# Row sums of the attention weights from two matmuls in place of three, in a two-layer cross-attention kernel

## What is computed

```python
# layer 0
scores = einsum('bqh,bkh->bqk', Q, K) * scale
x = query + einsum('bqh,hd->bqd', softmax(scores, -1) @ V, Wo) + bo
# layer 1: softmax over the QUERY axis (axis=1), so the rows of w do not sum to one
w = softmax(einsum('bte,bme->btm', q, k) * scale, axis=1)
pred = einsum('btm,bme->bte', w, v)          # v = latent @ Wv + bv
x = pred + emb
out = (x - mu) * rsqrt(var + EPS) * gamma + beta
```

## Time and profile before

| | |
|---|---|
| median of 3 runs | 1209.86 us (1209.61 to 1211.09) |
| the profiled execution's own time | 1209.69 us |
| its span, first to last instruction | 1207.9 us |
| mean granted TensorE clock | 0.982 |
| PE busy | 1159.0 us, 96% of the span |
| DVE busy | 883.6 us, 73% |
| ACT busy | 858.5 us, 71% |
| POOL busy | 968.5 us, 80% |

### The profile page before, as it was taken

One profiled execution on the slowest core, in us unless ns is written; L12 is line 12 of the kernel. 1 busy time (PEld: TensorE's weight loads), 2 busy tenths in 40 slices (PEclk: granted clock), 3 DMA queues, 4 the chain that ended last, 5 costly groups with the idle time before them and its releaser, 6 DMA issues.

```text
span 1207.9 us, 25274 instructions
## 1 busy us (share of the span) xinstructions
PE 1159.0 (96%) x7985; PEld 1078.0 (89%) x7985; DVE 883.6 (73%) x2061; ACT 858.5 (71%) x1736; POOL 968.5 (80%) x772
## 2 busy tenths in 40 slices
PE   6969999999999999999999999999999999999983
PEld 5659999999999999999999999999999999999873
DVE  0346787778777777777787778777877787777763
ACT  1436777777777777777777777777777777777752
POOL 1335888898889888988898889888888988898764
PEclk8989999999999999999999999999999999999997
DMA  8235666676667666766666666666666666676431
GB/s 347 68 117 187 227 212 219 216 238 204 223 210 238 201 224 216 231 203 226 218 224 206 228 221 220 212 226 226 212 218 215 237 207 223 209 243 201 155 123 53
DMA packets 131839, 250.09 MB, mean 207 GB/s; under 512 B 15712, under 2 KB 89440, under 8 KB 123232
## 3 DMA queue, kind: packets, MB, share of 16 engines
q1 hardware_dynamic: 130800, 248.64, 61.6%
q10 hardware_dynamic: 1008, 1.06, 0.2%
HBM read 165.68 MB, written 83.95 MB: 207 GB/s over the span
## 4 chain that ended last, share of the span: by engine, by line
PE 93%; DMA 2%; DVE 1%; ACT 1%; POOL 1%; issue 1%; ACTq 0%; POOLq 0%; DVEq 0%
PE bank L314 90%; PE bank L392 2%; DMA beta_b<-in_beta 1%; PE bank L429 1%; PE bank L423 1%; ACT bank L502 0%; DVE scol L826 0%; DVE stats L847 0%; PE bank L442 0%; DMA gT<-g_dram 0%; POOL PT_lo L954 0%; POOL Y L1010 0%; POOL yT_lo L954 0%; DVE R L839 0%; ACTq L507 0%
## 5 line engine op out<-in xcount | busy, mean ns | idle before, releaser
L954 POOL TENSOR_TENSOR xT_lo<-IN,xT_hi 128x1024 fp32r<-128x1024 f32 x64 | 154.3, 2411 | 27.9 <-ACT xT_hi L502 27.9
L954 POOL TENSOR_TENSOR yT_lo<-yT_raw,yT_hi 128x1024 fp32r<-128x1024 f32 x64 | 152.4, 2381 | 28.0 <-ACT yT_hi L502 26.6
L1010 POOL TENSOR_TENSOR Y<-Y,gamma_b 128x512 f32<-128x512 f32 x128 | 162.9, 1295 | 0.9 <-ACT Y L636 0.9
L1013 POOL TENSOR_TENSOR Y<-Y,beta_b 128x512 f32<-128x512 f32 x128 | 163.1, 1298 | 0.0
L636 ACT ACTIVATE Y<-R,nmr,rstd 128x512 f32<-128x512 f32 x128 | 97.5, 809 | 80.8 <-POOL nmr L1002 80.8
L1000 POOL TENSOR_TENSOR rstd<-ve,half 128x2 f32<-128x2 f32 x64 | 44.8, 700 | 133.1 <-DVE nmu L862 133.1
L314 PE MATMUL bank<-yT_hi,A_hi 128*128 128x256 f32 x512 | 145.5, 284 | 5.3 <-POOL yT_lo L954 5.3
L314 PE MATMUL bank<-xT_hi,A_hi 128*128 128x256 f32 x512 | 145.5, 284 | 0.0
L314 PE MATMUL bank<-xT_hi,A_lo 128*128 128x256 f32 x512 | 145.3, 284 | 0.0
L314 PE MATMUL bank<-yT_lo,A_hi 128*128 128x256 f32 x512 | 145.2, 284 | 0.0
L314 PE MATMUL bank<-xT_lo,A_hi 128*128 128x256 f32 x512 | 145.0, 283 | 0.0
(11 more groups left out here) (108 smaller groups left out, 4252.1 us busy)
## 6 DMA issues: line engine op xcount, KB each, us to landing
IN<-in_packed SPq DMA_DIRECT2D x64, 1024.0 KB, 4.9
R<-in_x SPq DMA_DIRECT2D x64, 512.0 KB, 4.4
y_dram<-y_blk SPq DMA_DIRECT2D x256, 128.0 KB, 2.6
yT_raw<-y_dram SPq DMA_DIRECT2D x64, 512.0 KB, 3.7
out<-Y SPq DMA_DIRECT2D x64, 512.0 KB, 2.6
E_dram<-E_blk SPq DMA_DIRECT2D x256, 64.0 KB, 1.8
PT_raw<-E_dram SPq DMA_DIRECT2D x64, 256.0 KB, 2.8
gT<-g_dram SPq DMA_DIRECT2D x64, 128.0 KB, 3.7
```

The lines of the kernel that those rows point to most:

```text
L954: return nc.gpsimd.tensor_tensor(dst, src, fp(hi), ALU.subtract)
L1010: nc.gpsimd.tensor_tensor(y[:, q, :], y[:, q, :], gamma_b[:, :], ALU.mult).then_inc(Y_mul, 1)
L1013: last = nc.gpsimd.tensor_tensor(y[:, q, :], y[:, q, :], beta_b[:, :], ALU.add)
```

## The change

The row sum over keys is `w_hi[0] + w_lo[0] + w_hi[1] + w_lo[1]`. The changed kernel adds the full weights of the two key tiles first and splits this sum once. ACT writes `w_1` (the weights of tile 1, not rounded); DVE computes `w_sum` = tile 0 times its reciprocal + `w_1`; ACT rounds `w_sum` to `w_sums_hi`; POOL subtracts to give `w_sums_lo`; PE's `s_` multiplies ones by these two. POOL's `w_low_sum` is gone. Besides, steps change places: `C_h` goes ahead of `wc_h` on ACT; on DVE `x2(r-1, 0)` goes ahead of `g_blocks`, `stats_ready` ahead of `rz1_`, and `x1(r+2, 1)` ahead of `w_l`; on POOL `cT_l` goes ahead of `scales`.

```diff
@@ PE @@
                 first(pe, s_set, n.count(back=1))
-                pe.wait_ge(w_los_set, n.count())
-                for t, part in enumerate((w[0][:, 0, :], w[0][:, 1, :], w_los[:, :])):
-                    last = nc.tensor.matmul(s_bank[:, 0:S], ones[:, :], part, start=(t == 0), stop=(t == 2))
+                pe.wait_ge(w_sums_lo, n.count())
+                for t, part in enumerate(w_sums):
+                    last = nc.tensor.matmul(s_bank[:, 0:S], ones[:, :], part[:, :], start=(t == 0), stop=(t == 1))
                 last.then_inc(s_full, 1)
@@ ACT @@
+            def w_1_(n):
+                if not n.there():
+                    return
+                act.wait_ge(rz1_set, n.count())
+                first(act, w_sum_set, n.count(back=1))
+                copy(w_1[:, :], S1_bank[:, S:2 * S], scale=rz1[:, 1:2]).then_inc(w_1_set, 1)
+
+            def w_sums_h(n):
+                if not n.there():
+                    return
+                act.wait_ge(w_sum_set, n.count())
+                first(act, s_full, n.count(back=1))
+                copy(w_sums[0][:, :], w_sum[:, :]).then_inc(w_sums_hi, 1)
...
                 if prefix:
+                    C_h(r.plus(3))
                     wc_h(r.plus(-1))
                     pred_seed_(r.plus(-1))
                     PT_h(r.plus(2))
                     u_h(r.plus(3))
-                    C_h(r.plus(3))
                 xT_h(r.plus(4))
...
                 w_h(r)
+                w_1_(r)
                 cT_h(r.plus(4))
+                w_sums_h(r)
                 normalise(r.plus(-1))
@@ DVE @@
+            def w_sum_(n):
+                if not n.there():
+                    return
+                dve.wait_ge(w_1_set, n.count())
+                dve.wait_ge(w_hi, n.count())
+                first(dve, w_sums_lo, n.count(back=1))
+                nc.vector.scalar_tensor_tensor(w_sum[:, :], S1_bank[:, 0:S], rz1[:, 0:1], w_1[:, :], ALU.mult, ALU.add
+                                               ).then_inc(w_sum_set, 1)
...
+                x2(r.plus(-1), 0)
                 g_blocks(r.plus(1))
-                x2(r.plus(-1), 0)
...
+                stats_ready(r.plus(-1))
                 rz1_(r)
-                stats_ready(r.plus(-1))
                 E0_blocks(r.plus(3))
                 variances(r.plus(-1))
                 x1(r.plus(2), 0)
+                w_sum_(r)
+                x1(r.plus(2), 1)
                 w_l(r)
-                x1(r.plus(2), 1)
@@ POOL @@
-            def w_low_sum(n):
-                if not n.there():
-                    return
-                pool.wait_ge(w_lo, n.count())
-                first(pool, s_full, n.count(back=1))
-                nc.gpsimd.tensor_tensor(w_los[:, :], fp(w[1][:, 0, :]), fp(w[1][:, 1, :]), ALU.add
-                                        ).then_inc(w_los_set, 1)
+            def w_sums_l(n):
+                if not n.there():
+                    return
+                pool.wait_ge(w_sums_hi, n.count())
+                minus(w_sums[1][:, :], w_sum[:, :], w_sums[0][:, :]).then_inc(w_sums_lo, 1)
...
+                cT_l(r.plus(4))
                 scales(r.plus(-1))
-                cT_l(r.plus(4))
-                w_low_sum(r)
+                w_sums_l(r)
```

More of the change, by code:

```diff
@@ L113, in build @@
         gT = sb("gT", [P, 1, S])
-        w_los = sb("w_los", [P, S], f32r)
+        w_1 = sb("w_1", [P, S])
+        w_sum = sb("w_sum", [P, S])
+        w_sums = split("w_sums", [P, S])
         scol = sb("scol", [P, ST, 32])
@@ L154, in build @@
         S1_seed, S1_full, nmax1_set, E1_set = sem("S1_seed"), sem("S1_full"), sem("nmax1_set"), sem("E1_set")
-        rz1_set, w_hi, w_lo, w_los_set = sem("rz1_set"), sem("w_hi"), sem("w_lo"), sem("w_los_set")
+        rz1_set, w_hi, w_lo = sem("rz1_set"), sem("w_hi"), sem("w_lo")
+        w_1_set, w_sum_set = sem("w_1_set"), sem("w_sum_set")
+        w_sums_hi, w_sums_lo = sem("w_sums_hi"), sem("w_sums_lo")
         s_full, s_set = sem("s_full"), sem("s_set")
```

## The result

The changed kernel takes 1230.39 us (median of 4 runs, 1228.81 to 1231.03), against 1209.92 for the kernel before (4 runs). The ratio is 1.016, with a 95% interval of 1.0145 to 1.0175: slower by 1.6%. The profiled execution took 1230.26 us, its span is 1228.5 us.

The account below looks back on a forecast made before the run. PE was taken as the bound, never waiting in mid-run, in 59 periods of 17.36 us. 1209.7 - 7.5 + 59 * 0.47 = 1229.9, +1 for the end: 1231 us, range 1210 to 1240.

Parts of the forecast that it names:

- The late seeds: Before `pred_`: scales 1.6 us late delay `vT`, `scol` and seeds; PE stalls 0.45 to 0.53 us a period, 0.47 taken.
- Waits that hang on one anchor do not add: Stalls before `wc_` and `pred_` both hang on `S0_`; the `w_lo` wait lies inside the 0.47 us.
- The late `w_lo`: Before `wc_`: `w_l` behind the second `x1` alone stalls PE 0.11 to 0.35 us a period, 0.26 taken, 0.20 possible.
- `PT_l` as a third chain: Before `Pc_`: later `Y` and `finish` delay `PT_l`; stall of 0.21 to 0.45 us, inside the seeds' stall.
- The price of the matmul: In `s_`: one of three matmuls goes in each of 64 sequences, 0.117 us each, saving 7.5 us.
- The number of periods and the end: 59 periods of 0.47 us stall each, and 1 us more in the last four sequences without a next sequence as cover.
- Only the matmul counts: Rival: the chain over `scales` has room, seeds arrive in time; 1202 us, stall below 0.12 us a period; chance 0.12.
- Only `w_l` stalls PE: Rival: POOL's order is harmless, PE waits before `wc_` only, 0.20 to 0.26 us a period; 1215 to 1219 us; chance 0.12.
- the fourth rival: Stalls of 0.1 to 0.17 us a period nearly cancel the gain; 1207.4 to 1212.3 us; chance 0.06.
- The clock: Rival: PE's pauses lower its clock, 2 us of each period at 1.2 GHz; about 1290 us; chance 0.02.

Follow-up runs that it names:

- 1: The changed kernel with POOL running `scales` ahead of `cT_l` again: 1221.25 us, ratio 1.0088.
- 8: The kernel before with `cT_l` ahead of `scales` on POOL and the added copy `w_1` on ACT, its result unused: 1232.33 us, ratio 1.0183.
- 9: The changed kernel with the copy `w_1` on ACT made twice, the first into an unread buffer: 1253.6 us, ratio 1.0359.
- 4: The changed kernel with `C_h` put back behind `u_h` on ACT: 1230.58 us, ratio 1.0165.
- 2: The changed kernel with `w_l` ahead of the second `x1` on DVE, behind `w_sum_`: 1231.65 us, ratio 1.0166.
- 3: The changed kernel with `scales` first on POOL and `w_l` ahead of the second `x1` on DVE: 1205.74 us, ratio 0.996.
- 11: The changed kernel with every step in the order of the kernel before, `w_l` directly behind `w_sum_`: 1205.87 us, ratio 0.9962.
- 6: The kernel before with `w_l` behind the second `x1` on DVE: 1214.28 us, ratio 1.0024.
- 5: The kernel before with `cT_l` ahead of `scales` on POOL: 1214.19 us, ratio 1.0025.
- 7: The kernel before with `cT_l` ahead of `scales` on POOL and `w_l` behind the second `x1` on DVE: 1213.44 us, ratio 1.0022.

## Why the prediction was right

**The forecast.** 1231 us was said, 1230.39 measured; slower by 1.7% was said, 1.6% measured. The period was to be 17.24 + 0.47 = 17.71 us; it is 17.69. The mechanism holds; that the total is as close as 0.6 us is luck in part (see the sizes below).

**The late seeds.** Right in every link. With the shift of 8.26 us, predicted and measured starts: `cT_hi` 603.04 and 603.04, `cT_lo` 603.76 and 603.77, `rstd` 605.02 and 605.03, `vT_hi` 607.44 to 607.52 and 607.53, `scol` 608.68 to 608.76 and 608.75, the seeds 609.81 to 609.89 and 609.87. The experiments take each part away: POOL's order (1), the copy (8, 9), `C_h` as no part of it (4). The text of the prediction named `wc_h` behind `C_h` in following ACT, but let the seeds start behind the columns; experiment 4 shows that this was the right one of the two.

**Waits that hang on one anchor do not add.** The prediction did not add the wait for `w_lo` to that for the seeds. Experiments 1 to 3 show it: the late `w_lo` alone costs 0.27 us a period, and the late seeds alone (0.43) cost as much as both together (0.44). In the change the larger part of the loss is even seen at `wc_` (0.23 us there and 0.18 at `pred_`, which is all but 0.03 of the 0.44), but the seeds set its size: what PE loses at `wc_` it need not wait at `pred_`. Adding them would have given 0.47 + 0.26 = 0.73 us a period and about 1246 us.

**The late `w_lo`.** Taken at 0.26, possible at 0.20 if `stats_ready` helped; experiment 1 measured 0.27 by itself, a little above. `E_blk` does start 0.06 us sooner (610.37 - 8.26 = 602.11, against 602.17), but in some of the loop's bodies DVE's timeline has longer gaps behind it (from `nmu` to the first `x1` 0.24 us in the period that ends at 598, 0.10 in the next), which takes it back. In those periods more of the loss is at `wc_`: of four periods in a row, 0.28, 0.15, 0.39 and 0.14 us are lost there, and 0.16, 0.27, 0.04 and 0.26 at the `pred_` that follows.

**`PT_l` as a third chain.** POOL's `finish` waits 0.31 us for `Y` as foreseen (the row of `gamma_b` above); it starts at 607.00 with the shift taken off, where 606.9 was said. But neither the change nor experiments 2 and 3 show a wait for `PT_lo` in mid-run. It stays inside. That it would have come next was only argued.

**The price of the matmul.** Mis-sized: 0.117 us from a step of 0.35 for three, measured 0.107. The removed part is 6.8 us, not 7.5.

**The number of periods and the end.** 59 periods * 0.33 us (17.69 - 17.36) = 19.7 us; the spans differ by 20.6. From the `s_` at 1146.58 to the end are 81.9 us, against 79.9 from the one at 1128.00 before: +2.0, where +1 was said. Against that, the first `s_` comes 1.1 us earlier (102.66 against 103.76). So four sizes were off by 1 to 2 us each: the matmuls give 59 * 0.107 = 6.3 us and not 7.5, the stall is 17.69 - 17.25 = 0.44 us and not 0.47 (26.0 us in place of 27.7), the end costs 2.0 and not 1, and the earlier first `s_`, 1.1 us, was not in the sum. Together -6.3 + 26.0 + 2.0 - 1.1 = 20.6 us, where the prediction had -7.5 + 27.7 + 1 = 21.2. That the errors nearly cancel is luck.

**The rivals.** "Only the matmul counts" is what happens without the two orders (3, 11). "Only `w_l` stalls PE" is what happens with scales first (1). The bounds of the first and the fourth rival overlap: a stall of 0.1 to 0.12 us a period belongs to both as they are written; with 0.44 measured this decides nothing. The clock stayed at 1.00 mid-run (the columns are PE's busy time, matmuls, granted clock, DMA share, GB/s):

```profile
100.00:1100.00 1000.00, 998.27 (x6896) 1.00 0.64 214
```

The Trainium skill, page "TensorE: Matmul & The Clock Gate", section "A second HAM failure mode: psum-queue depth-cycling", describes another kernel, in which short pauses made the clock swing. Here one or two pauses of 0.1 to 0.4 us in each period of 17.7 us did not: the granted clock of this stretch is 1.00. Near the end of the run it is otherwise. The prediction read from the earlier trace rows that a pause of 1.93 us had not brought the lower level; in experiment 6 a pause of the same length, in the same place, is followed by it (last section), so that one row was weak evidence. And a 512-wide matmul then takes 0.43 us from start to start, not the 0.46 that the prediction put for it.

## What to carry to other kernels

When one engine is the bound and is never waited for, find the latest link of every chain that ends at it, and sum the queue positions along it. The busy shares (73% on ACT and DVE here) say nothing: 0.36 us on ACT in the wrong place cost 0.35 us in every period (9), and the same operation in a chain with room cost nothing there (3, 11). A reordering that is nearly free in one kernel (0.02 us a period) can be what makes the next addition cost nearly its whole length (0.33 of 0.36 us), so order and addition must be tried together and apart. Among waits that start from the same anchor only the longest counts; removing the shorter one shows nothing until the longer is gone.

## What the runs showed that I had not expected

The end of the run, where no new sequences follow and PE waits more (the drain), can differ by 3 to 4 us between profiled executions of kernels whose periods are alike (from the last `s_` of the 59 periods to the end: 79.9 us before, 82.8, 83.7 and 83.3 in experiments 5, 6 and 7). Experiments 5, 6 and 7 are 0.2% slower than before, of which their periods explain 1.1 to 1.8 us. Most of the rest is in the steps of the last sequences. The chain that ended last has a block of 84 matmuls there, first in the kernel before, then in experiment 6:

```profile
1147.80 13.21 PE bank L314 x84
```

```profile
1148.89 14.79 PE bank L314 x84
```

It took 14.79 us in place of 13.21, and from 1145 to 1165 us the granted clock was 0.91 in place of 0.96:

```profile
1145.00:1165.00 20.00, 16.14 (x100) 0.96 0.53 159
```

```profile
1145.00:1165.00 20.00, 17.10 (x104) 0.91 0.52 172
```

The seeds ahead of it reach PE after the same 0.83 to 0.84 us in both, and PE waited the same 1.93 us. Two neighbouring matmuls of the block in experiment 6:

```profile
1149.74 0.63 PE L314 MATMUL bank<-V_hi,wcT_hi 128*128 128x512 f32 x1
1150.17 0.63 PE L314 MATMUL bank<-V_lo,wcT_hi 128*128 128x512 f32 x1
```

The step is 0.43 us; between the same two matmuls of the kernel before (1148.58 and 1148.81) it is 0.23. Seven steps in a row are of that length, with one of 0.31 ahead of them and one of 0.35 behind; from 1153.08 on the pace is that of the kernel before. These steps are the whole 1.58 us of the block. So two executions that drain alike differ by how much of the drain runs at the lower clock level (1.2 in place of 2.4 GHz). Part of that is not the kernel's: the 23 executions of the kernel before that ran beside experiments 5 and 6 took from 1208.55 us (mean granted clock 0.983) to 1213.01 us (0.981). The kernels differ as well, with all 12 executions of experiment 5 at 1212.79 us or more and a clock of 0.981 or less; why it is more in experiments 5 to 7 stays open. With a bound of 0.2% for "no change", the prediction's, this lies at the edge of what can be told.
